# Layer 4's attention in units of one batch and two heads, its value product from split operands, and the next unit's scores ahead of the values

## The reference, cut to what matters

```
def _L3_xattn_ref(latents, context, Wq, Wk, Wv, Wo):      # latents: layernorm(x), context: 8 x 128 x 512
    hidden_states = jnp.concatenate([context, latents], axis=1)           # 256 keys
    q = (latents @ Wq).reshape(b, 128, 4, 8, 128)          # 32 heads of 128, 4 groups of 8
    k = (hidden_states @ Wk).reshape(b, 256, 4, 128)
    v = (hidden_states @ Wv).reshape(b, 256, 4, 128)       # one k and v for each group of 8 heads
    attn = softmax(einsum('bqhgd,bkhd->bhgqk', q, k) / sqrt(128))
    out = einsum('bhgqk,bkhd->bqhgd', attn, v)
    return out.reshape(b, 128, 4096) @ Wo
x = x + tanh(g_xattn[3]) * _L3_xattn_ref(_layernorm(x), ctx_4096, ...)
x = x + tanh(g_ffn[3]) * _L3_ffn_ref(_layernorm(x), ...)   # 6-bit weights, dequantised
```

## Time and profile before

| | |
|---|---|
| median of 3 runs | 2762.68 us (2758.4 to 2764.48) |
| the profiled execution | 2762.54 us, its span 2760.7 us |
| PE busy | 2682.1 us, 97% of the span |
| PEld busy | 2264.1 us, 82% |
| DVE busy | 1776.6 us, 64% |
| ACT busy | 1122.1 us, 41% |
| POOL busy | 839.7 us, 30% |
| chain that ended last | PE 91%, DVE 6%, ACT 1% |
| granted TensorE clock, mean | 0.993 of full speed |

### The profile page before, as it was taken

The page is one execution under the profiler, slowest core; times in us unless marked ns, Lnnn a source line. Parts: engine busy times, 40 slices in busy tenths (PEclk is TensorE's granted clock), DMA queues, the critical chain, the costliest instruction groups (busy, mean ns, idle before and its releaser), DMA issues.

```text
span 2760.7 us, 45251 instructions
## 1 busy us (share of the span) xinstructions
PE 2682.1 (97%) x14736; PEld 2264.1 (82%) x14736; DVE 1776.6 (64%) x3493; ACT 1122.1 (41%) x3088; POOL 839.7 (30%) x715
## 2 busy tenths in 40 slices
PE   6998999999999999999999999999999999999998
PEld 5886888888888887777888888788878888888887
DVE  5766545546446447777999999845553666666667
ACT  3542433333333333135666666421123444444442
POOL 4003433334324424323223222245523222222200
PEclk9999999999999999999999999999999999999999
DMA  5002111101101101111111111012211101110000
GB/s 149 17 5 67 43 35 50 38 29 51 42 23 53 42 27 46 37 38 39 31 34 30 34 30 33 29 47 61 58 45 40 28 28 28 32 28 28 28 5 31
DMA packets 59789, 106.01 MB, mean 38 GB/s; under 512 B 7184, under 2 KB 11536, under 8 KB 59536
## 3 DMA queue, kind: packets, MB, share of 16 engines
q1 hardware_dynamic: 56448, 96.49, 12.5%
q10 hardware_dynamic: 3216, 7.81, 0.8%
HBM read 100.09 MB, written 2.10 MB: 37 GB/s over the span
## 4 chain that ended last, share of the span: by engine, by line
PE 91%; DVE 6%; ACT 1%; issue 1%; POOL 1%; DMA 0%; DVEq 0%; ACTq 0%; POOLq 0%
PE four L651 50%; PE outp L651 25%; PE value L651 9%; PE turned L1016 4%; PE turned L773 1%; DVE stats L1703 1%; DVE x L1970 1%; PE value L698 0%; PE turned L698 0%; DVE probs L1732 0%; DVE nt L1665 0%; DMA raw<-in_stream 0%; PE turned L651 0%; DVE xt_lo L1737 0%; DVE probs L1850 0%
## 5 line engine op out<-in xcount | busy, mean ns | idle before, releaser
L614 POOL TENSOR_TENSOR w_hi<-raw,zero 128x512 fp32r<-128x512 f32 x347 | 372.6, 1074 | 1742.7 <-PE four L651 569.0
L1970 DVE SCALAR_TENSOR_TENSOR x<-outp,g_inv,x 128x512 f32<-128x512 f32 x768 | 548.6, 747 | 329.5 <-PE outp L651 328.6
L618 POOL TENSOR_TENSOR w_lo<-raw,w_hi 128x512 fp32r<-128x512 f32 x352 | 455.6, 1294 | 31.3 <-ACT w_hi L1304 4.2
L651 PE MATMUL four<-xt_hi,w_lo 128*128 128x512 f32 x1024 | 428.0, 418 | 3.9 <-DVE xt_lo L1737 3.2
L651 PE MATMUL four<-xt_hi,w_hi 128*128 128x512 f32 x1024 | 403.1, 394 | 0.0
L651 PE MATMUL four<-xt_lo,w_hi 128*128 128x512 f32 x1024 | 401.7, 392 | 0.0
L651 PE MATMUL outp<-w_hi,a_lo 128*128 128x512 f32 x800 | 327.1, 409 | 19.6 <-DVE a_lo L2069 10.4
L651 PE MATMUL outp<-w_hi,a_hi 128*128 128x512 f32 x800 | 316.7, 396 | 0.0
L651 PE MATMUL outp<-w_lo,a_hi 128*128 128x512 f32 x800 | 316.3, 395 | 0.0
L1519 ACT ACTIVATE probs<-probs,top 128x128 f32<-128x128 f32 x512 | 199.6, 391 | 213.6 <-DVE top L2014 127.4
L1304 ACT ACTIVATE pT<-turned 128x512 f32<-128x512 f32 x320 | 193.1, 603 | 203.4 <-PE turned L1016 145.6
(11 more groups left out here) (299 smaller groups left out, 4911.1 us busy)
## 6 DMA issues: line engine op xcount, KB each, us to landing
raw<-in_stream SPq DMA_DIRECT2D x352, 256.0 KB, 2.6
ctx_raw<-in_ctx_t ACTq DMA_DIRECT2D x4, 512.0 KB, 6.2
x<-in_x_in ACTq DMA_DIRECT2D x2, 1024.0 KB, 10.6
kz<-kT SPq DMA_DIRECT2D x32, 64.0 KB, 2.7
pb<-in_position_bias ACTq DMA_DIRECT2D x1, 2048.0 KB, 9.2
out<-x SPq DMA_DIRECT2D x8, 256.0 KB, 2.0
qw<-in_qweight ACTq DMA_DIRECT2D x1, 768.0 KB, 3.9
ln_w<-in_ln_weight ACTq DMA_DIRECT2D x1, 256.0 KB, 2.6
```

What stands on the lines that cost most here:

```text
L614: pool.tensor_tensor(w_hi[:, k, :], raw[:, k % RAW, :], zero[:, :].to_broadcast([P, D]), ALU.add)\
L618: pool.tensor_tensor(w_lo[:, k, :], raw[:, k % RAW, :], f32(w_hi[:, k, :]), ALU.subtract)\
L651: m = pe.matmul(out_, l, r, start=start, stop=stop, skip_group_check=True)
L1970: dve.scalar_tensor_tensor(out=x[:, b, :], in0=O[no_f(k) % 2][:, :], scalar=scale, in1=x[:, b, :], op0=ALU.mult, op1=ALU.add)\
```

## The change

It alters layer 4's attention alone.

- A unit is one batch and two heads (`U = 8`, `together = 2`), still 128 units of two output tiles. Both tiles of a unit are added to the same rows of x. Four query slots of 512 columns instead of two; three query pieces instead of two in the prologue.
- `values(k-1)` uses split operands: two `mm3` of 256 columns (both heads side by side), 6 matmuls instead of 4 fp32 ones. ACT's copy from bank T gives `pT_hi` (128x512, as before); new on DVE is `turned_lo` (`pT_lo`, 128x512 from the bank), once a unit. New on DVE is also `values_split` (v of two batches of a group, a rounding copy and a subtraction), in steps 0, 2, 4 and 6 of each 32, 16 times in all. `v_hi` lies over `kT` and `v_lo` over `v`.
- `scores(k+1)` stands in step k, between `output(k-2)` and `values(k-1)`.
- DVE's order in a step: `top(k)`, the factor of unit k-1, `turned_lo(k-1)`, `keys_split`, `values_split`, the adds, `a_lo`, `q_lo`. Before, `keys_split` came ahead of the factor. It stands in steps 31, 33, 35 and 37 of the first group and 32 on for the next two.
- New waits: `turn` for the last `pT_lo`; `values` for its `pT_lo` and its `v` split; the second add for the first; `turned_lo` for `pT_hi`.
- The scale of the first four tiles' norm behind the attention is worked out in step 127 instead of 128. The feed-forward bias is loaded in step 34 instead of the prologue.

```diff
@@ Attention.__init__
+        self.together = 2 if name == "L3" else 1
-        self.NU = heads * units
+        self.NU = heads // self.together * units
-        self.nb = B // units
+        self.nb = self.together * B // units
...
-            order = [("k", 0, pair) for pair in range(4)] + [("q", 0, 0), ("q", 0, 1)]
-            for i in range(self.NU):
-                order += self.keys_split(i) + self.pieces(i)
+            order = [("k", 0, pair) for pair in range(4)] + self.first[-self.ahead:]
+            for i in range(self.NU + 1):
+                order += [("pT", i - 1)] if i else []
+                order += self.keys_split(i) + self.values_split(i) + self.pieces(i)
...
@@ Attention: pieces and splits
-        return [("q", t // 2, t % 2 * 2, 2)]
+        return [("q", self.query_piece(i)[1], i % 2 * 2, 2)]
+    def query_piece(self, i):
+        group, odd = divmod(i // 2 + self.ahead, 2)
+        return 2 * (group // 2) + odd, group % 2
...
     def keys_split(self, i):
-        group, pair = divmod(i + 1, 8 * self.U)
-        return [("k", group, pair)] if i + 1 < self.NU and group and pair < 4 else []
+        group, at_ = divmod(i + 1, 4 * self.U)
+        return [("k", group, at_ // 2)] if i + 1 < self.NU and group and at_ in (0, 2, 4, 6) else []
+    def values_split(self, i):
+        group, at_ = divmod(i, 4 * self.U)
+        return [("v", group, at_ // 2)] if i < self.NU and at_ in (0, 2, 4, 6) else []
...
-       Attention("L2", HEADS, 2, 8), Attention("L3", HEADS, 4, 0)]
+       Attention("L2", HEADS, 2, 8), Attention("L3", HEADS, 8, 0)]
@@ PE: scores, turn
-                        pe.wait_ge(s["split"], max(L.split[("q", h, t // 2)], L.split[("k", h // 8, t)]))
+                        heads, m, b = L.unit_heads(k), k // (4 * L.U), t
+                        pe.wait_ge(s["split"], max([L.split[("k", m, b // 2)]]
+                                                   + [L.split[("q", hd, b // 4)] for hd in heads]))
...
                         pe.wait_ge(s["pT"], at(L, lambda i: i, k, it))
+                        if n == 3:
+                            pe.wait_ge(s["split"], L.split[("pT", k - 1)])
...
@@ PE: values, step
+                        group, b = k // (4 * L.U), k % L.U
+                        pe.wait_ge(s["split"], max(L.split[("pT", k)], L.split[("v", group, b // 2)]))
+                        for kt in range(2):
+                            both = slice(kt * 2 * P, (kt + 1) * 2 * P)
+                            m = mm3(V[:, 0:2 * P], (v_hi(group, b)[:, tokens(kt)], v_lo(kt, b, group)),
+                                    (buf["pT_hi"][:, both], buf["pT_lo"][:, both]), kt == 0, kt == 1, last=kt == 1)
...
-                    if k < L.NU:
+                    if k < L.NU and (k == 0 or n not in SCORES_FIRST):
                         scores(k, it)
...
                         output(k - L.lag_o, it)
+                    if k + 1 < L.NU and n in SCORES_FIRST:
+                        scores(k + 1, it)
                     if L.has_V(k):
@@ ACT
-                        copy(buf["pT"][:, 0, :], T[:, :]).then_inc(s["pT"], 1)
+                        copy(buf["pT_hi"][:, :] if n == 3 else buf["pT"][:, 0, :], T[:, :]).then_inc(s["pT"], 1)
...
+                    if n == 3 and k == 4 * L.U + 2:
+                        act.dma_start(M3["bias"], q_bias).then_inc(phase_in["F3"], 16)
@@ DVE
+                def values_split(what):
...
+                    dve.tensor_copy(hi, v).then_inc(s["split"], 1)
+                    dve.wait_ge(s["split"], L.split[what] - 1)
+                    dve.tensor_tensor(lo, v, f32(hi), ALU.subtract).then_inc(s["split"], 1)
+                def turned_lo(u):
+                    dve.wait_ge(s["pT"], u + 1)
+                    dve.tensor_tensor(buf["pT_lo"][:, :], T[:, :], f32(buf["pT_hi"][:, :]), ALU.subtract)\
+                        .then_inc(s["split"], 1)
...
+                        back = B if n < 3 else 1 if j else 2 * B - 1
...
-                        if no_f(k) > B:
-                            dve.wait_ge(s["x_acc"], at(L, lambda i: no_f(i) - B, k, it))
+                        if no_f(k) > back:
+                            dve.wait_ge(s["x_acc"], at(L, lambda i: no_f(i) - back, k, it))
...
+                        if n == 3 and k == L.NU - 1:
+                            norm_scale(range(B // 2), ln_base(norm + 1) + 6)
                         if n == 3 and k == L.NU:
-                            norm_scale(range(B // 2), ln_base(norm + 1) + 6)
                             norm_rows(norm + 1, 0)
...
-                    if n == 3 and k < L.NU:
+                    if 1 <= k <= L.NU:
+                        scaled_gate(k - 1, it, small)
+                    if n == 3:
+                        if 1 <= k <= L.NU:
+                            turned_lo(k - 1)
                         for what in L.keys_split(k):
                             keys_split(what)
-                    if 1 <= k <= L.NU:
-                        scaled_gate(k - 1, it, small)
+                        for what in L.values_split(k):
+                            values_split(what)
                     through(k, it, small)
```

More of the change, by code:

```diff
@@ L79, in early_chunks, with batches @@
         return []
+    def batches(self, i):
+        return list(range(B))
 class Attention:
@@ L111, in __init__ @@
                 u = i - self.lag_o
-                for b in self.batches(u):
-                    self.tile[(u, b)] = len(self.tile) + 1
+                for j in range(self.nb):
+                    self.tile[(u, j)] = len(self.tile) + 1
                 if u % self.U == self.U - 1:
-                    self.order.append(("o", u // self.U))
+                    self.order += [("o", h) for h in self.unit_heads(u)]
             if name == "L2":
@@ L198, in parts, with slot, unit_heads @@
             return ahead + [("q", 1 - t, 0, 1), ("q", 1 - t, 1, KT - 2), ("q", 1 - t, KT - 1, 1)]
-        return [("q", t // 2, t % 2 * 2, 2)]
+        return [("q", self.query_piece(i)[1], i % 2 * 2, 2)]
+    def query_piece(self, i):
+        group, odd = divmod(i // 2 + self.ahead, 2)
+        return 2 * (group // 2) + odd, group % 2
+    def slot(self, what):
+        _, h, t = what
+        return (2 * (h // 2 * 2 + t) + h % 2) % 4
+    def unit_heads(self, i):
+        first = self.together * (i // self.U)
+        return list(range(first, first + self.together))
     def made_head(self, i, kind="q"):
+        if self.name == "L3":
+            return self.query_piece(i)[0]
         if self.name == "L1" and kind == "k":
@@ L351, in build @@
             M3["u"] = sb("u", [P, KT, D], I32, st)
-        M3["bias"] = sb("q_bi", [P, D])
-        sb("behind_bias", [P, (KT - 1) * D])
+        q_lo = sb("q_lo", [P, 4, HALF], F32R)
         with ExitStack() as st:
@@ L381, in attention_buffers @@
         def attention_buffers(stack, n):
-            queries = {"qT": sb(f"qT{n}", [P, 2, TOK], F32, stack)} if n < 3 else \
-                {"q_hi": sb("q_hi", [P, 2, HALF], F32R, stack), "q_lo": sb("q_lo", [P, 2, HALF], F32R, stack)}
+            if n == 3:
+                return {
+                    "q_hi": sb("q_hi", [P, 4, HALF], F32R, stack),
+                    "q_lo": q_lo,
+                    "pT_hi": sb("pT_hi", [P, D], F32R, stack),
+                    "pT_lo": sb("pT_lo", [P, D], F32R, stack),
+                    "a_hi": sb("a_hi3", [P, 2 * P], F32R, stack),
+                    "a_lo": sb("a_lo3", [P, 2 * P], F32R, stack),
+                }
             return {
-                **queries,
+                "qT": sb(f"qT{n}", [P, 2, TOK], F32, stack),
                 "pT": sb(f"pT{n}", [P, 1, D], F32, stack),
@@ L1433, in leave_bank @@
                     if kind == "q" and n == 3:
-                        dst, scale = buf["q_hi"][:, part, :], q_scale_
+                        dst, scale = buf["q_hi"][:, L.slot(what), :], q_scale_
                     elif kind == "q":
```

72 lines of the change are left out of this document (49 added, 23 removed).

## The result

The changed kernel takes 2766.47 us (median of 20 runs, 2763.06 to 2769.49), the kernel before 2762.02 in the 20 runs beside them (2757.69 to 2765.15): a ratio of 1.0016, interval 1.0009 to 1.0023. The 4.4 us are slower by sign, clear of the noise by the interval, and inside the prediction's band for no change (0.2%) by size. The forecast was 2755.4, with a range from 2743 to 2766; the measured time lies just above it, and 11 us above the forecast.

What follows compares the result with a forecast made beforehand. PE, busy all 590 us of the stage, was taken as the bound. Value product -23.0, key-split stalls +11.2 and last steps +4.7 sum to -7.1, so 2762.54 becomes 2755.4 us, range 2743 to 2766.

Steps and rivals of the forecast that it cites:

- The value product: Values on PE, each step: six float32r matmuls replace four fp32, 0.89 to 0.71, over 128 units -23.0 us.
- The rows: Profile times of the scores, six matmuls of the same shape: they put the value product at 0.71, a fifth less.
- the pass count: Skill's rule of four passes for true FP32: value columns 2048 to 1536, 0.89 to 0.67, a gain of 28 us.
- What DVE gets: DVE in the stage: turned_lo 77 us, later second add 14, value splits 17; 7.3 of 9.3 us per two steps, fits.
- ordinary and value-split steps: Mid-stage steps: pT_lo ready with 0.49 us of cover; a_lo 0.35 late after value splits without output waiting; cost 0.
- Key-split steps: Steps 31, 33, 35, 37 and their like: scores wait for k_lo, 0.67 + 3 x 1.02 a group, +11.2, bounds 0 to +20.
- SP's and POOL's queues have room: Weight stream through the ring: same chunks, POOL busy 132 of 590 us, so cost 0.
- The last steps: Six steps without a query piece, output waiting for a_lo: 4.18 each, cost +4.7 with the prologue's piece, bounds 0 and +8.
- the moved piece: One query piece run in the prologue instead of late in the stage: same PE work, 2.8 us there.
- The norm's scale: DVE's 2.2 us of scale work, one step earlier, before the last turned_lo: taken as 0, between -2.2 and +2.2.
- The clock: Rival, slower: last six steps might run at 1.2 GHz, 3.25 more each, about +20, 2775 us; chance 0.06.
- the key splits stay hidden: Rival: key splits cost PE nothing, as before; 2762.5 - 23.0 + 4.7 = 2744 us; chance 0.13.

Runs made afterwards that it cites:

- e2: Changed kernel with POOL's weight splits withheld in steps 31 to 37 of each group, key splits where they were; 2757.89 us, ratio 0.9981.
- f3: Changed kernel, scores still ahead of values, key splits two steps earlier and POOL's weight splits held back through step 38; 2743.61 us, ratio 0.9931.
- e1: Changed kernel with each key split of groups 1 to 3 two steps earlier, nothing else; 2755.24 us, ratio 0.9974.
- f2: Changed kernel, scores behind values again, POOL's weight splits held back through step 38, turned_lo ahead of top in the last six steps; 2744.54 us, ratio 0.9932.
- e3: Changed kernel with the scores back at the head of their step, behind the values, split value product kept; 2746.71 us, ratio 0.9945.

## Why the prediction was wrong

Point by point, by its own steps:

- **The value product** (0.89 to 0.71, 0.18 a step, -23.0): right. 0.89 is now 0.72 and the step 4.66; the 121 steps gained 21.0 of 21.8. The rows were the better guide than the pass count that I had weighed against them: a fifth was gained, not a quarter.
- **What DVE gets; ordinary and value-split steps at 0**: right. In the stage PE waits for no `pT_lo`, and DVE is at 478.4 / 586.2 = 82% (84% forecast).
- **Key-split steps** (0.67 + 3 x 1.02 a group, +11.2, at most +20): this is the step that failed. The place, the twelve waits and the order of the chain were right, and so, nearly, was the size of what I had counted (11.2, and 10.05 measured in e2; the way from DVE to PE, which the working has at 0.26, is 0.05 to 0.06 from the end of `k_lo` to the matmul in all twelve steps). The term of the sum was +23.7, outside its bound of +20, because the durations, 0.42 and 0.69, came from rows in which POOL happened to be idle. So it was for all twelve key splits of the kernel before (0.42 and 0.69 each), and not by a wide margin: the one ahead of the earlier trace rows ended 0.32 ahead of a POOL burst (`k_lo` started at 2253.71 and took 0.69):

```profile
2254.72 1.04 POOL L614 TENSOR_TENSOR w_hi<-raw,zero 128x512 fp32r<-128x512 f32 x1 [5.79 <-PE outp L651]
```

  The change moved the two onto each other.
- **"SP's and POOL's queues have room: 0"**: wrong in kind. I weighed POOL's time as capacity, 132 of 590 us, and never as a neighbour at the same ports. e2 takes away the stretch, and in its trace the lower clock is gone with it: 9.7 us less than the changed kernel (1.0016 - 0.9981 of 2762), with some 4 of its own on top. f3 shows it from the other side: e1's -7 became -19 when POOL was kept out as well.
- **The last steps** (4.18 each, +4.7 with the moved piece): right within 0.1 a step (4.09 to 4.10). That the difference is right to 0.1 us (+0.8 and +0.7) is partly luck: the six steps took 24.6 us where 25.1 were forecast, and 23.9 before where the working has 24.3, so two errors of 0.4 to 0.5 cancel. The profile names `a_hi` for the wait of 0.54; the output needs `a_lo` too, which follows `a_hi` and ends 0.11 ahead of the output (2711.94 and 2712.05), so the forecast's wait for `a_lo` is the one that ends last.

```profile
2712.05 0.47 PE L699 MATMUL outp<-w_hi,a_lo 128*128 128x512 f32 x1 [0.54 <-ACT a_hi L1370]
```

- **The norm's scale**, 0 between -2.2 and +2.2: it did get in the way of the last `turned_lo` (the values of the last unit wait 2.26 us for it), and the stretch behind unit 127 is nevertheless 1.1 shorter, within what executions differ by. So its worth is not shown either way.

```profile
2724.13 0.36 PE L699 MATMUL value<-pT_hi,v_lo 128*128 128x256 f32 x1 [2.26 <-DVE pT_lo L1998]
```

- **The clock** was put down as a rival with its place in the last six steps, where it stayed up. It fell inside the stage of the profiled execution, behind long stalls, and cost 4.7 us. The Trainium skill (TensorE: Matmul & The Clock Gate, section A second HAM failure mode: psum-queue depth-cycling), by which frequent micro-idles let the clock oscillate, is borne out in part only: e2 has twelve stalls of up to 0.93 at clock 1.00 throughout, and the changed kernel's drops stand behind stalls of 2.2 to 2.3. The same stalls did not always do it. In the first group the clock fell behind the second of the two, in the second group not at all (steps 63 and 65 took 6.97 and 6.89, all at 1.00), and in the third already behind the first, in step 95, and again behind the second:

```profile
2559.60:2567.28 7.68, 5.64 (x31) 4.76 (x29) 6.12 (x10) 2.49 (x7) 2.36 (x2) 0.89 0.12 34
2567.28:2572.79 5.51, 5.51 (x30) 4.87 (x29) 4.68 (x10) 2.00 (x6) 0.00 (x0) 0.84 0.00 0
```

  In e1 step 34 has 2.24 us of idle PE, in two pauses of 1.51 and 0.73, and the clock stays up:

```profile
2261.76:2269.13 7.37, 5.13 (x30) 4.11 (x29) 7.16 (x12) 2.01 (x6) 4.93 (x4) 1.00 0.35 89
```

  What exactly lets the clock fall no run here took apart.
- **The rival "the key splits stay hidden", 2744**, is what f2 and f3 measure, 2744.5 and 2743.6. The rest of the sum therefore holds; only what the hidden splits need, the earlier notice and POOL out of the way, was not in the change.

## What to carry to other kernels

The duration of an instruction in one trace holds for its neighbours in that trace: before a VectorE cast, `tensor_scalar` or operation on two SBUF tiles is put on the critical path, look up which GpSimd instructions can run beside it, and price it as ending behind them (0.28 us behind for the cast here, 0.55 for the subtraction). Moving a consumer forward cost 3.0 us here and adding work ahead of its producer gained 15.2, and the two together cost 4.4, so the notice that a producer has left is to be computed with both in. GpSimd work that is released by another engine's progress can be held back for a few steps as long as its ring has the stock, but the burst that is then let go must not meet the next such instruction: in e2 that cost 4.2 us.

## What the runs showed of the hardware

- A VectorE cast from SBUF to SBUF or a subtraction of two SBUF tiles (128x512) that starts while a GpSimd split of 128x512 fp32 (1.04 and 1.3 us alone) runs ends a fixed time behind it: the cast 0.28, the subtraction 0.55, in 53 of 53 cases. How long it lasts thus depends on where it starts: in these traces the cast lasts 0.74 to 1.28 instead of 0.42, the subtraction 1.41 to 1.67 instead of 0.69, and a `tensor_scalar` of 128x2, which ends 0.02 behind, up to 1.29 instead of 0.23. Not all is stretched: subtractions with one PSUM operand (`pT_lo`) stay at 0.68 to 0.69, and the reciprocal of 128x2, which is in SBUF alone, at 0.15 to 0.16 in 150 cases beside POOL.
- Where VectorE starts first, by as little as 0.05 us, it keeps its time, and the GpSimd instruction pays: 1.04 becomes 1.48 in step 33 of the changed kernel and 1.53 in e3.
- A stall of 2.2 to 2.3 us was followed by a granted clock of 0.5, the lower of the two levels (1.2 GHz), in three of six cases; step 34, of which a part ran so, took 6.25 instead of 4.66. With stalls of 0.93 no such step was seen.
- Six float32r matmuls of 256 columns cost the same 0.71 to 0.72 as scores or as values, and against four fp32 ones of 128 columns (0.89) save a fifth.
